# Second feed-forward: the eviction of the turned inner rows moves behind the squares of its ScalarE step

## The reference

```
def activation_quant(x):
    scale = 127.0 / jnp.clip(jnp.max(jnp.abs(x), axis=-1, keepdims=True), EPS_Q, None)
    return jnp.clip(jnp.round(x * scale), -128, 127) / scale
...
def bitlinear(x, norm_w, w):
    x_norm = rmsnorm(x, norm_w)
    x_q = x_norm + jax.lax.stop_gradient(activation_quant(x_norm) - x_norm)
    w_q = w + jax.lax.stop_gradient(weight_quant(w) - w)
    return jnp.einsum('bsd,hd->bsh', x_q, w_q)
h = bitlinear(x, norm1_w, w1)
h = act_scale * jnp.square(jax.nn.relu(h)) + act_bias
y = bitlinear(h, norm2_w, w2)
return y
...
x = x + _L1_ffn_ref(_layernorm(x, axis=-1), ...)
```

## Time and profile before

| | |
|---|---|
| median of 3 runs | 1326.2 us (1320.96 to 1332.5) |
| profiled execution | 1329.82 us, span 1328.0 us |
| mean granted TensorE clock over the span | 0.927 |
| busy over the span | PE 84%, DVE 69%, ACT 41%, POOL 39% |
| last stage, 1190 to 1300 us | 110 us: PE 75.55, DVE 90.49, ACT 93.63, POOL 72.23 us busy, clock 0.89 |

### The profile page before, as it was taken

One profiled execution on the slowest core, in us unless ns is written; L12 is line 12 of the kernel. 1 busy time (PEld: TensorE's weight loads), 2 busy tenths in 40 slices (PEclk: granted clock), 3 DMA queues, 4 the chain that ended last, 5 costly groups with the idle time before them and its releaser, 6 DMA issues.

```text
span 1328.0 us, 30836 instructions
## 1 busy us (share of the span) xinstructions
PE 1113.8 (84%) x9234; PEld 783.1 (59%) x9234; DVE 917.8 (69%) x2318; ACT 539.3 (41%) x953; POOL 515.1 (39%) x875
## 2 busy tenths in 40 slices
PE   3699999999997889898864888988888889776675
PEld 2577777777775565665542465656565656534443
DVE  2646666666664575767564788888888888478886
ACT  1332322222222211111132355555555555568886
POOL 0324444444442122222103144444444444366664
PEclk7699999999998999999987799999999999868988
DMA  9323222233331000000027866666665666540000
GB/s 218 106 90 88 87 87 87 87 88 92 91 93 47 1 1 0 0 0 0 1 57 153 157 132 137 130 131 134 128 137 126 142 124 131 161 150 24 24 24 32
DMA packets 121314, 116.07 MB, mean 87 GB/s; under 512 B 45076, under 2 KB 114231, under 8 KB 121271
## 3 DMA queue, kind: packets, MB, share of 16 engines
q1 hardware_dynamic: 121270, 115.55, 36.4%
HBM read 79.15 MB, written 36.00 MB: 87 GB/s over the span
## 4 chain that ended last, share of the span: by engine, by line
PE 52%; DVE 19%; ACT 8%; issue 8%; SPq 5%; DMA 4%; POOL 2%; DVEq 1%; ACTq 0%; POOLq 0%
PE bank L1484 23%; PE bank L1642 6%; DVE nm L1270 5%; PE bank L1740 3%; PE bank L1578 3%; PE bank L1754 3%; PE bank L1724 3%; ACT v_all L995 2%; ACT v_all L988 2%; DVE npart L1279 2%; DVE hT L1189 2%; ACT v_all L982 2%; DMA qs<-mrow 2%; PE bank L1567 2%; DVE yn L1178 1%
## 5 line engine op out<-in xcount | busy, mean ns | idle before, releaser
L1270 DVE TENSOR_REDUCE nm<-bank 112x1 f32<-112x375 f32 x512 | 257.8, 539 | 47.1 <-PE bank L1724 44.3
L943 ACT ACTIVATE pT<-bank 125x448 f32<-125x448 f32 x384 | 192.2, 542 | 103.9 <-PE bank L1754 77.6
L1724 PE MATMUL bank<-ks,qs 96*128 96x375 bf16 x512 | 170.7, 347 | 21.5 <-DMA qs<-q_parts_dram 18.4
L1740 PE MATMUL bank<-qs,ks 128*128 128x112 bf16 x1536 | 143.8, 218 | 8.6 <-DMA qs<-mrow 7.8
L1740 PEld LDWEIGHTS bank<-qs,ks 128*128 128x128 bf16 x1536 | 104.2, 101 | 44.2 <-issue 29.5
L1754 PE MATMUL bank<-pT,vaug 125*32 125x112 f32 x3072 | 116.5, 270 | 0.0
L1642 PE MATMUL bank<-wffT,hT 128*112 128x256 f32 x384 | 100.7, 396 | 0.0
L894 ACT ACTIVATE yT<-bank,bcol,gcol 128x448 f32<-128x448 f32 x48 | 32.2, 721 | 163.4 <-PE bank L1624 163.4
L1754 PEld LDWEIGHTS bank<-pT,vaug 125*32 125x32 f32 x3072 | 68.8, 111 | 38.2 <-issue 34.1
L1484 PE MATMUL bank<-wv1T,ctxT 128*125 128x256 f32 x384 | 88.0, 379 | 0.0
L1484 PE MATMUL bank<-ctxT,wk1T 128*128 128x375 f32 x256 | 86.0, 478 | 0.0
(11 more groups left out here) (204 smaller groups left out, 2343.6 us busy)
## 6 DMA issues: line engine op xcount, KB each, us to landing
k_parts_dram<-kp SPq DMA_DIRECT2D x192, 93.8 KB, 3.5
ks<-k_parts_dram SPq DMA_DIRECT2D x64, 281.2 KB, 4.2
cnat<-in_ctx_dram SPq DMA_DIRECT2D x32, 375.0 KB
ks<-k_parts_dram SPq DMA_DIRECT2D x64, 187.5 KB, 3.9
ks<-k_parts_dram SPq DMA_DIRECT2D x64, 93.8 KB, 3.3
q_parts_dram<-qp SPq DMA_DIRECT2D x48, 112.0 KB, 2.2
qs<-q_parts_dram SPq DMA_DIRECT2D x64, 84.0 KB, 4.0
x_stream<-in_x_dram SPq DMA_DIRECT2D x4, 896.0 KB, 13.8
```

The lines of the kernel that those rows point to most:

```text
L943: act.activation(pT[:, u % 4, :], B3[u % 3][0:TP], ACT.Exp).then_inc(probs_made, 1)
L1270: dve.tensor_reduce(nm[:, h:h + 1], A3[h % 3][0:L], AX_X, ALU.max, negate=True).then_inc(head_max_taken, 1)
L1724: mm(A3[h % 3], qs[par][0:KS, h * L:h * L + P], ks[par][0:KS, h * T:(h + 1) * T], start=True, stop=True).then_inc(max_scores_made, 1)
L1740: last = mm(B3[c][:, j * L:(j + 1) * L], ks[par][:, h * T + c * TP:h * T + c * TP + P], qs[par][:, h * L:(h + 1) * L], start=True, stop=True)
```

## The change

In ScalarE's step the inner eviction `hq_out(i - 2)` is issued third instead of first. Each wait goes with its instruction. The dependencies between tiles are as before.

```
             def step4(i, par, n):
-                if not isinstance(i, int) or i >= 2:
-                    hq_out(i - 2)
                 if not isinstance(i, int) or i < NT - 2:
                     xq_out(i + 2, par)
                 if not isinstance(i, int) or i < NT:
                     squares(i, par)
+                if not isinstance(i, int) or i >= 2:
+                    hq_out(i - 2)
                 if not isinstance(i, int) or i < NT - 1:
                     relu(i + 1, 1 - par)
                     square(i + 1, 1 - par)
```

## The result

The changed kernel takes 1361.8 us (median of 4 runs, 1359.6 to 1366.1), the kernel before 1327.9 beside it: a ratio of 1.0269, 95% interval 1.0239 to 1.0299; the two medians lie 33.8 us apart. The forecast was 58.3 more and a range of 1349 to 1395. The direction, the mechanism of the first term and the range held; the second term, the clock's, was over three times too large.

A forecast was written before the change was run, and what follows sets the result against it. The closing chain through ScalarE, VectorE and TensorE bounds the last stage at 5.48 us a step. Slower steps 55.0, first step 2.4 and end 0.9 sum to + 58.3 on 1326.2: 1384.5 us, range 1349 to 1395.

The forecast's parts named there:

- Term 1, ScalarE's own loop: Second feed-forward: the moved eviction adds 0.92 us to ScalarE's loop, 5.47 to 6.39 us a step.
- Term 2, TensorE's loop: Second feed-forward: products and turns queue behind the moved eviction, 6.04 us a step at full clock, 8.36 at half.
- How often is the clock low?: Second feed-forward steps: clock falls more often, returns later; 8.0 us a step, 55.0 us more over 22 steps.
- a clock above 0.85: Sign against the prediction: the last stage's mean clock staying above 0.85 instead of falling from 0.89 to about 0.6.
- the step from 1171.45: Earlier profile's step at clock 0.50 throughout, TensorE busy 4.55 of 5.72 us; model for the 8.0 us estimate.
- the clock holds: Rival for the last stage: TensorE stays near 2.4 GHz, only term 1 counts, + 22.9 us, 1349; chance 0.33.
- its variants with 22% and 40% of the time at half: The held-clock rival with 22% or 40% of the time at half clock: 1359 or 1366 us.
- the case that was forecast: Clock mostly low in the last stage's steps: 1366 to 1397 us, chance 0.57.
- The rule of the Trainium skill's page: TensorE idling briefly between matmul groups can swing between clocks; alone, the whole stage goes at 8.36 us a step.
- an eviction hidden at its new place: Rival on ScalarE: the moved eviction fits free before a waiting relu, its old place is freed; 1325 us, chance 0.06.
- The small terms: First step with an inner eviction + 2.4 us; path behind tile 27's outer eviction + 0.9 us.
- The tail's clock: After tile 27's outer eviction: an allowance of 0, give or take 3 us.

The follow-up runs named there:

- The extra copy: Kernel before, order untouched, plus one unread 128x1024 ScalarE copy of the square behind the squares of steps 2 to 27: 1353.4 us, ratio 1.0214.
- the filled gap with the eviction in place: Changed kernel plus 16 unread 128x256 matmuls on TensorE ahead of the second product: 1351.3 us, ratio 1.0198.
- the kernel with the rounding first: Changed kernel with VectorE's rounding of the outer tile ahead of the activation of its step: 1359.9 us, ratio 1.0250.
- both of these loops opened: Changed kernel with VectorE's rounding ahead of the activation and TensorE's first product ahead of its second: 1324.0 us; with 8 unread matmuls between the products, 1321.7 us.
- Half of a move: Kernel before with the inner eviction moved behind the squares in the even steps only: 1358.0 us, ratio 1.0242.
- The kernel before with the rounding first: Kernel before with VectorE's rounding of the outer tile ahead of the activation: 1319.7 us, ratio 0.9956.

## Why the prediction was right, and where it was not

*Term 1, ScalarE's own loop: right.* 6.38 us measured against 6.39; over 22 steps 19.4 us against 19.6. The extra copy shows it by itself (6.41 us in most steps), and the filled gap with the eviction in place.

*Term 2, TensorE's loop: the mechanism right.* The loop through both products exists (5.68 us at the full clock in the kernel with the rounding first; 6.04 had been worked out, from whole durations where starts follow sooner). Filling the gap takes 10.7 us off the 22 steps, exchanging the products 9.6 (141.35 us against 150.97), and both remove the steps above 6.7. A first step of 7.95 us against 8.36 forecast is this loop too.

*"How often is the clock low?": the step that failed.* I put the mean step at 8.0 us, four fifths of the way to half the clock throughout, and the stage's mean clock at about 0.6. It came to 6.86 and 0.84; a clock above 0.85 had been named as a sign that the prediction is wrong, and that was missed by a hundredth. In the sum the clock's part was 55.0 - 19.6 = 35.4 us and measured 10.5. Two things were too high: how many steps have a fall (8 of the 22 have none), and what such a step costs (0.6 to 0.9 us over 6.38 instead of 1.97). The second is seen in the timeline above: the clock is back by the inner turns, so only the products pay.

The argument was a likeness to the step from 1171.45, which stays at half the clock with TensorE busy 4.55 of 5.72 us. But the work of that step lies in pieces with gaps of 0.48, 0.25 and 0.45 us between them, while the new order puts products and turns in one piece. The share of work isn't alike either: 0.80 there, 5.8 of 8.36 or 0.69 in the forecast step. And the earlier trace rows show the clock coming back in the very next step, behind products and turns in one piece: inner turns of 1.69 us, where the step before has 1.97, then outer turns of 0.44 instead of 0.69. So the likeness didn't hold, and the rows before had shown as much. Which of these differences decides how soon the clock comes back, and why some steps have no fall, is open: no run changes one of them alone.

*The rivals.* What happened is nearer to "the clock holds": its variants with 22% and 40% of the time at half gave 1359 and 1366, and the measured third of the time lies between them, as 1361.8 does. In that agreement there is luck: the variants took the share of time for the share of steps and each such step at 1.97 us. A third of the time makes 22.9 + 0.32 x 1.97 x 22 = 36.8 us more by them and 33.1 were measured, from 14 of 22 steps at some 0.75 us. The rival had a chance of 0.33 against 0.57 for the case that was forecast. The rule of the Trainium skill's page "TensorE: Matmul & The Clock Gate" that was weighed (section "A second HAM failure mode: psum-queue depth-cycling") is borne out in kind: the clock swings between its two levels (0.84 in the mean), and with the gap filled it doesn't (1.00). That page of the Trainium skill tells it of another kernel, which cycles through PSUM banks; here the gap is a wait for an eviction. Taken alone the rule gave 8.36 us a step, and 6.86 were measured. The rival on the other side, an eviction hidden at its new place, has nothing for it: relu and eviction start without any idle time.

*The small terms.* First step + 1.98 against + 2.4, end + 0.84 against + 0.9. The tail's clock moved nothing beyond that.

## What to carry to other kernels

An engine's idle hole that belongs to the closing chain is free room; the stretch on either side of it is not, and moving an operation of 1 us out of the one into the other costs its start-to-start distance in every step. Before such a move, look also at what is queued behind its consumer: here the first product and both turns stood behind the second product, and exchanging the two products took back some 10 of the 34 us with the eviction where it is. With both of these loops opened a third appeared, two steps long, through the order of VectorE's queue. Half of a move need not cost half.

## What the runs showed of the hardware that I had not expected

Matmuls of no use made a kernel faster: 16 of them in a gap of 2.68 us took the mean clock of 22 steps from 0.84 to 1.00, and those steps together are 10.7 us shorter. In the kernel before, whose two gaps of 1.1 us took up the slow products, 8 of them took the mean clock of the 22 steps from 0.90 to 1.00, and a step is 0.04 us shorter. The kernel before with the rounding first, which has no fill and steps of 5.05 us, stood at 1.00 in all 22 steps as well. With the gap in every other step the clock fell in all of the long steps; with it in every step, in about two of three.
